# Two attentions, a quantised feed-forward network and an expert layer on one core: seven stages with a barrier between each, and the same stages in fewer blocks with their tiles interleaved

## The reference

```python
x = x + _L0_xattn_ref(_layernorm(x), ctx_768, Wq, bq, Wk, bk, Wv, bv, Wo, bo)      # 16 heads of 16
x = x + _L0_ffn_ref(_layernorm(x), w_gate, w_up, w_down)
x = x + _L1_xattn_ref(_layernorm(x), ctx_768, mask, g_norm, null_kv, Wq, Wkv, Wout, g_out)  # 16 heads of 64
x = x + _L1_ffn_ref(_layernorm(x), W, b, Wg, bg)                                   # 8 experts, top 2
```

```python
x = act_qdq(x)                              # scale = max|x| / 32767
up = act_qdq(x @ lpbq_dequant(w_up).T)
gate = act_qdq(x @ lpbq_dequant(w_gate).T)
sig = fixed_qdq_u16(jax.nn.sigmoid(gate))
gate = act_qdq(gate * sig)
o = act_qdq(gate * up)
return o @ lpbq_dequant(w_down).T
```

## Time and profile before

| | us |
|---|---|
| median of three runs | 1203.74 |
| the profiled execution | 1201.73 |
| its span in the profile | 1200.0 |
| PE busy | 1092.3 |
| DVE busy | 954.8 |
| ACT busy | 602.0 |
| POOL busy | 473.6 |

### The profile page before, as it was taken

One profiled execution on the slowest core, in us unless ns is written; L12 is line 12 of the kernel. 1 busy time (PEld: TensorE's weight loads), 2 busy tenths in 40 slices (PEclk: granted clock), 3 DMA queues, 4 the chain that ended last, 5 costly groups with the idle time before them and its releaser, 6 DMA issues. The chain is left out here.

```text
span 1200.0 us, 19905 instructions
## 1 busy us (share of the span) xinstructions
PE 1092.3 (91%) x6208; PEld 902.4 (75%) x6208; DVE 954.8 (80%) x2563; ACT 602.0 (50%) x1337; POOL 473.6 (39%) x546
## 2 busy tenths in 40 slices
PE   7899999996898885895997899999999969999997
PEld 5677777885786664442996898889989858888786
DVE  4688998886685989897664888988888759888886
ACT  1566766773555887586781333433433323333332
POOL 1245445432000757674000444555554434343433
PEclk9899999998899998687898999999999979999999
DMA  9000000000233686597204011011000000000000
GB/s 275 1 2 1 1 1 1 1 2 1 106 119 127 220 291 245 162 350 266 88 1 144 21 44 45 1 45 45 1 1 1 1 1 19 18 17 17 26 18 26
DMA packets 50048, 82.56 MB, mean 69 GB/s; under 512 B 4636, under 2 KB 35696, under 8 KB 49968
## 3 DMA queue, kind: packets, MB, share of 16 engines
q1 hardware_dynamic: 48591, 80.77, 19.9%
q10 hardware_dynamic: 1376, 0.79, 0.3%
HBM read 45.65 MB, written 35.90 MB: 68 GB/s over the span
## 5 line engine op out<-in xcount | busy, mean ns | idle before, releaser
L1134 PE MATMUL a_ps<-VW,a_PT 128*128 128x256 f32 x640 | 143.5, 379 | 0.0
L1134 PEld LDWEIGHTS a_ps<-VW,a_PT 128*128 128x128 f32 x640 | 120.2, 190 | 15.0
L1172 ACT ACTIVATE a_U<-a_U 128x1280 f32<-128x1280 f32 x32 | 40.7, 1271 | 110.7 <-DVE a_U L1257 110.7
L2245 POOL TENSOR_TENSOR m_half<-m_half 128x512 f32<-128x512 f32 x32 | 41.2, 1286 | 130.6 <-ACT m_half L2207 130.6
L1151 ACT COPY a_PT<-a_ps 128x512 f32<-128x512 f32 (+1 forms) x96 | 46.0, 517 | 82.6 <-PE a_ps L1097 82.6
L2147 PE MATMUL m_ps<-m_wh,m_xh 128*128 128x512 f32 x256 | 86.6, 420 | 0.0
L915 DVE TENSOR_SCALAR a_U<-a_ps 128x320 f32<-128x320 f32 x128 | 59.2, 484 | 32.8 <-PE a_ps L723 21.5
L1850 POOL TENSOR_SCALAR f_sg<-f_sg 128x1024 f32<-128x1024 f32 x24 | 36.7, 1529 | 113.6 <-ACT f_sg L1807 113.2
L2147 PE MATMUL m_ps<-m_wl,m_xh 128*128 128x512 f32 x256 | 80.9, 398 | 0.0
L1249 DVE TENSOR_REDUCE a_mx<-a_ps 128x4 f32<-128x320 f32 x128 | 62.4, 488 | 22.8 <-PE a_ps L1084 22.4
L2147 PE MATMUL m_ps<-m_wh,m_xl 128*128 128x512 f32 x256 | 80.6, 396 | 0.0
(11 more groups left out here) (257 smaller groups left out, 3179.6 us busy)
## 6 DMA issues: line engine op xcount, KB each, us to landing
up_scratch<-f_ub SPq DMA_DIRECT2D x24, 512.0 KB, 3.0
f_ul<-up_scratch SPq DMA_DIRECT2D x24, 512.0 KB, 5.5
key_scratch<-p_keys SPq DMA_DIRECT2D x8, 640.0 KB, 6.7
vw_scratch<-p_vw SPq DMA_DIRECT2D x16, 320.0 KB, 5.7
k_raw<-key_scratch SPq DMA_DIRECT2D x8, 640.0 KB, 6.1
VW<-vw_scratch SPq DMA_DIRECT2D x4, 1280.0 KB, 5.7
xs<-in_x SPq DMA_DIRECT2D x4, 1024.0 KB, 12.4
h_scratch<-f_hh SPq DMA_DIRECT2D x8, 512.0 KB, 2.7
```

Of the source, the lines that this page charges most:

```text
L1134: last = pe.matmul(Y[:, 0:D], PTs[t.p][:, j, :], fold.values[t.batch % 2][:, j, :], start=(j == 0), stop=(j == NJ - 1))
```

## The change

**Stages 4, 6 and 7 of the kernel become one block.** The last feed-forward stage, the second attention and the expert layer no longer write their programs themselves; each returns a `Stage` of generators, one for each engine, that yield after each step, and `finish` draws from them in an order given by hand. `d`, `a` and `m` are the three stages; the number is of steps.

```diff
+def finish(nc, down, att, experts):
...
+    with nc.Block() as block:
+        @block.sync
+        def _(sp):
+            down.sync(sp)
+            att.sync(sp)
+            experts.sync(sp)
+        @block.tensor
+        def _(pe):
+            d, a, m = down.tensor(pe), att.tensor(pe), experts.tensor(pe)
+            steps(d, 28)
+            steps(a, 3)
+            steps(d, 2)
+            steps(a, 1)
+            steps(d, 2)
+            steps(d)
+            steps(a, NT)
+            steps(m, 3)
+            steps(a, 1)
+            steps(m, 1)
+            steps(a)
+            steps(m)
...
+        @block.vector
+        def _(dve):
+            d, a, m = down.vector(dve), att.vector(dve), experts.vector(dve)
+            steps(d, 28)
+            steps(a, 2)
+            steps(d, 4)
+            steps(a, 1)
+            steps(d, 2)
+            steps(a, 1)
+            steps(d)
+            steps(a, 1 + NT - 2)
+            steps(m, 1)
+            steps(a, 1)
+            steps(m, 1)
+            steps(a, 1)
+            steps(m, 1)
+            steps(a, 1)
+            steps(m, 1)
+            steps(a)
+            steps(m)
```

**The down products** are written out on PE for all chunks. In the first chunk the units are outside and the token tiles inside, and the first unit goes through ACT and DVE in two halves:

```diff
+        def tensor(pe):
+            def down(t, j, u, ks):
+                for o_, w_ in ((oh, dTh), (ol, dTh), (oh, dTl)):
+                    for k in ks:
+                        lhs = o_[t % 2][:, u, k * CW + j * P:k * CW + (j + 1) * P]
+                        last = pe.matmul(Y[j][:, 0:D], lhs, w_[:, 2 * u + k, :],
+                                         start=(u == 0 and o_ is oh and w_ is dTh and k == 0),
+                                         stop=(u == UC - 1 and w_ is dTl and k == 1), skip_group_check=True)
+                return last
+            def ready(t, u):
+                pe.wait_ge(s_oh, UC * t + u + 1)
+                pe.wait_ge(s_ol, UC * t + u + 1)
+            pe.wait_ge(s_half[1], 1)
+            pe.wait_ge(s_half[2], 1)
                     for j in range(TC):
-                        if t.t0 >= 1:
-                            pe.wait_ge(s_x2, t.of(lambda n: TC * (n - 1) + j + 1))
-                        n = 0
+                down(0, j, 0, (0,))
+            ready(0, 0)
+            for j in range(TC):
+                down(0, j, 0, (1,))
+            for u in range(1, UC):
+                ready(0, u)
+                for j in range(TC):
+                    last = down(0, j, u, (0, 1))
+                    if u == UC - 1:
+                        last.then_inc(s_dn, 1)
+                        yield
+            for t in range(1, NCH):
+                for j in range(TC):
+                    pe.wait_ge(s_x2, TC * (t - 1) + j + 1)
                         for u in range(UC):
                             if j == 0:
-                                pe.wait_ge(s_oh, t.of(lambda n: UC * n + u + 1))
-                                pe.wait_ge(s_ol, t.of(lambda n: UC * n + u + 1))
-                            for o_, w_ in ((oh, dTh), (ol, dTh), (oh, dTl)):
-                                for k in (2 * u, 2 * u + 1):
-                                    lhs = o_[t.p][:, u, (k % 2) * CW + j * P:(k % 2) * CW + (j + 1) * P]
-                                    last = pe.matmul(Y[j][:, 0:D], lhs, w_[:, k, :], start=(n == 0),
-                                                     stop=(n == 3 * MF - 1))
-                                    n += 1
+                            ready(t, u)
+                        last = down(t, j, u, (0, 1))
                         last.then_inc(s_dn, 1)
-                pipeline(pe, body, 0, NCH - 1, 2, 5)
-    return fold
+                    yield
```

**Feed-forward stages 2 and 3 become one block**, and the folding runs one step ahead of the products. PE after the last up products:

```diff
+                def folded(m):
+                    p1.folded_key(pe, m, 0)
+                    p1.folded_key(pe, m, 1)
+                    if m == 1:
+                        pe.wait_ge(s_sc, SCALED)
+                    if m >= 1:
+                        p1.folded_value(pe, m - 1, 0)
+                    p1.folded_key(pe, m, 2)
+                    p1.folded_key(pe, m, 3)
+                    if m >= 1:
+                        p1.folded_value(pe, m - 1, 1)
+                pe.wait_ge(s_ue, MF * NCH)
+                p1.query_T(pe, 0, 0)
+                p1.query_T(pe, 0, 1)
+                p1.key_product(pe, 0)
+                p1.key_product(pe, 1)
+                p1.value_product(pe, 0)
+                folded(0)
                 rows_max(pe, 2)
                 rows_max(pe, 3)
                 spread_max(pe, 2)
                 spread_max(pe, 3)
+                for m in range(1, NM):
+                    p1.value_product(pe, m)
+                    if m + 1 < NM:
+                        p1.key_product(pe, m + 1)
+                    folded(m)
+                p1.folded_value(pe, NM - 1, 0)
+                p1.folded_value(pe, NM - 1, 1)
+                rows_max(pe, 4)
+                spread_max(pe, 4)
```

1537 lines of the change are left out of this document (810 added, 727 removed).

## The result

| us | before | after |
|---|---|---|
| median | 1205.09 (4 runs, 1201.26 to 1207.77) | 1176.84 (4 runs, 1173.82 to 1182.60) |
| profiled execution | 1201.73 | 1173.82 |
| its span | 1200.0 | 1172.1 |

What follows compares the result with a forecast made beforehand. PE was taken to bound the kernel, losing time at the seams between blocks. Six terms summed to -27.2 us, so 1174.5 for a profiled execution and, with 2.0 added for the median, 1176.5 us; range 1165 to 1190.

Steps and rivals of the forecast that it cites:

- term 6: Seam from second attention to experts: lost time regained except new waits of 4.0 and 2.8 us; -9.0 us, bounds -12 and -5.
- Rival A: Expert entry: the clock falls in the new 4.0 us wait; +3.5 us, 1180; chance 0.15.
- Term 3: Seam from stage 2 to 3 and all of stage 3: late maxima, less entry work, shorter tail; -2.7 us, bounds +4 and -7.
- rival B: Seam of stages 2 and 3 loses: maxima or value weights late, tail gives less; +7 us, 1183; chance 0.13.
- Term 4: Start of stage 4: halved first unit, barrier gone, less waiting in first chunk; -3.3 us, bounds -4.4 and -1.7.
- Term 5: Seam from stage 4 to second attention: overlap removes idle time and lower clock; -11.7 us, bounds -13.7 and -7.6.
- Terms 1 and 2: Masks moved behind tile 28 of the first attention, +1.5 us; stage 2's queue without value and output weight loads, -2.0 us.
- Rival C: Both seams give half, DVE being the bound or waits acting as barriers; 1187 us; chance 0.06.
- Rival D: Last feed-forward stage: 576 written-out matmuls issue more slowly than the loop's 0.121 us each; slower, 1210 us; chance 0.03.

Runs made afterwards that it cites:

- the combined kernel: Changed kernel with the expert entry reordered on POOL, DVE, PE and ACT, and the masks moved from tile 28 to tile 30; 1166.64 us, ratio to before 0.9695.

## Why the prediction was right or wrong

**The failed step is term 6**, the seam from the attention to the experts: -9.0 predicted, -1.1 measured, outside its own bounds of -12 and -5. "PE stands 4.0 us" was worked out from DVE's queue alone. I walked PE's and DVE's order, and took POOL's reciprocal root for one of the small operations, without asking what stands ahead of it in POOL's own program. There stood a whole step of attention tile 30, which waits for DVE: +2.4 us; with that step moved the wait was 3.57, within the 4.0 that I had counted. The second wait was 3.25 for 2.8, +0.5. Then the two clock drops, +4.6 us. Together 7.5 of the 7.9 missed. The prediction had named a sign for a wrong sum, over 10 us of idle time of PE at the two seams: it was 12.5 (2.8 and 9.7). So by its own test the sum is wrong, though the total agrees.

**Rival A**, the clock falling in that wait, came true, and the time was still the forecast's: the price I gave it (+3.5) for the first drop alone was near the 3.0 measured there (5.9 us of work at half the clock), but the second drop was not foreseen. What I held against it, that 0.5 us less would do, was wrong: it fell with 3.57 and with 3.25 us as well. It held through the 2.51 us of the kernel with the low halves moved, but also through 3.28 us in the kernel with the addition on POOL (1.00 in each microsecond from 960 to 968, the wait ending at 964.20), so the length of the wait alone does not tell. The 2.9 us that I read for the first seam are 2.8: a mean of 0.87 in the microsecond from 646 puts the fall at 646.74, against 643.97. In the same way the 2.4 us of the expectation for POOL's moved step are 2.0 (936.2 against 934.2). The total hit because terms 3 and 4 and the start gave more. That each wait is paid anew, as the Trainium skill has it (TensorE: Matmul & The Clock Gate, section HAM oscillation), the trace of after bears out twice in 20 us, and the wait of 3.28 us just named does not; here the wait is one for another engine, where the page's case is one for a DMA.

**Term 3**, stages 2 and 3: -2.7 predicted, -8.9 measured, outside the bound of -7. Its parts: the late maxima cost 3.0 and not 5.0; the value weights came in time, and rival B did not come. The tail gave its 4.1 exactly. The mis-sized part is the products. For the first seven I took the mean of before's products 8 to 24, 2.99 us, as a floor, where they came in 18.5 us, 2.64 each: -6.0 in place of -3.6. For the later ones I had 0; they gave -1.8, at (548.81-502.75)/16 = 2.88 each. But the kernel with the moved gain wait, whose code is that of before there, has 2.88 as well, so these 1.8 are not shown to be the change's. From the two profiles, masks of 1.9 us (the six DVE operations of the earlier trace rows) and some 1.4 us of the first folding step's masks, which now lie ahead of the maxima in stage 2, left DVE's program there; DVE's waits between the first and the last product went from 5.6 to 3.5 us, and the products themselves from 36.2 to 33.4. That makes 8.2 less, of which 7.8 arrive. The last part is not the change's: in the kernel with the moved gain wait the products take 34.1. This split is read, not tested; only the null copy was, and it shows no part in it. So why the products came faster than forecast stays open in part.

**Term 4**: -4.3 against -3.3. Two mistakes in opposite directions: the barrier did not go (+0.5), and the first chunk gave 2.9 where I had 0.9: besides the waiting that went, the clock was up 3.3 us after PE's start and not 7.8, which I had only as a doubt in the bounds (1.2 to 3.1 over all kernels, so that 2.9 is a good draw). The halves gave 1.5 for my 1.9.

**Term 5**: the last chunk and the entry gave -11.8 for -11.7, with 2.8 us of waits left as predicted; chunks 2 to 7 took 1.2 more, of which 0.80 is one wait at 570.04 for `f_o`. The size is right, the reason in part not. I put all of the lost time down to the missing overlap; 3.2 to 3.5 us of it were a load that POOL waited for, which a look at POOL's first row of that stage would have told.

**Terms 1 and 2**: +1.7 and -2.1, near +1.5 and -2.0. The second has the cause that I gave, ACT's waits for the stores of up, which went from 8.4 to 4.0 us. But I had only one side of it: up to the last product of the stage it is -3.9 (83.9 for 87.7; 83.4 to 86.3 in the nine other kernels with the queue of after), and the three mask operations of the first folding step, ahead of the maxima now, took 1.8 back (5.2 for 3.4). The masks stand on PE as one wait for DVE. Timeline of PE, before and then after:

```profile
275.00 0.81 PE L723 MATMUL a_ps<-keys,a_qT 64*128 64x320 f32 x4 [0.76 <-DVE a_U L915]
```

```profile
273.90 1.34 PE L842 MATMUL a_ps<-keys,a_qT 64*128 64x320 f32 x4 [2.30 <-DVE a_U L1034]
```

That is 1.5 us more, the forecast. The whole stretch grows by 1.8 between the kernels in which the clock falls early and stays low (227.1 and 228.8 to 228.9). In after the clock besides dips right behind this wait (mean 0.76 from 272 to 276 and 0.82 from 276 to 280), which none of the kernels without the masks there shows, but falls for good only 1.8 us ahead of the end of the stretch, where before had 5.6. So +1.7 is partly luck, and with masks the last tiles can grow by more than the 2 us that I had named as a sign of being wrong: 2.8 to 3.1 against before in three kernels. Moved to tile 30 the masks cost nothing: 227.0 in the combined kernel, where the clock falls early too.

**Rival C** (the seams give half) did not come: the second seam gave even less than its 5.0, and the first all that was forecast. **Rival D** is refuted: 54 written-out matmuls from 613.75 to 620.24 come every 0.120 us, and the loop of before had 0.121.

## What to carry to other kernels

Where two stages are woven together by hand, write down for the first tile of the new stage the whole chain over all engines, small operations too, and read for each link what stands ahead of it in that engine's queue; a 0.55 us operation, queued behind another tile's step on an engine with time to spare, made 2.9 of the 6.4 us that PE stood here. A wait for a load that stands ahead of a loop costs as much as one in it: before overlapping two stages, look at the first row of each engine in the second. And a total that agrees proves no term: cut both traces at the same instructions and compare stretch by stretch.

## What the runs showed of the hardware

**The tail of the first attention has two lengths, with the same code.** Its last tiles leave PE gaps of 0.5 to 1.5 us, and in some executions the clock falls there. Stretches of the kernel with the moved gain wait:

```profile
276.00:280.00 4.00, 2.52 (x20) 2.21 (x20) 1.72 (x8) 3.17 (x11) 1.27 (x2) 1.00 0.00 0
280.00:284.00 4.00, 4.00 (x25) 3.97 (x24) 1.18 (x4) 0.00 (x0) 0.00 (x0) 0.65 0.00 0
284.00:288.00 4.00, 3.27 (x14) 2.69 (x13) 1.31 (x6) 1.82 (x4) 1.28 (x2) 0.50 0.00 0
```

and of before, which has the same code there:

```profile
284.00:288.00 4.00, 3.10 (x26) 2.81 (x26) 1.64 (x7) 1.63 (x4) 1.28 (x2) 1.00 0.01 4
```

In before it fell only in the last tile. The rest of the first attention takes 221.8 us there, and 227.1 where it falls at 281. With the code of the change it takes 223.5 in after and 224.6 to 224.9 in three other kernels; in these four the clock dips for 3.4 to 6.8 us behind the masks, comes back, and falls for good 1.8 to 6.2 us ahead of the end of the stretch. It takes 228.8 to 228.9 in five kernels, in which the clock does not dip behind the masks but falls 19 us ahead of the end and stays low. These 5.3 us, with the 4.4 between the earliest and the latest start, are as wide as the spread of one kernel's runs (1173.82 to 1182.60 for after), and they are why the experiments are compared by stretches. What decides in which executions the clock falls, no run here tells.

**The clock can fall after the wait is over.** At the second seam it fell in the microsecond from 956, after PE had resumed at 955.93 from a wait of 3.25 us; in the kernel with POOL's step moved it fell in the microsecond from 943 after a wait of 3.57 us that had ended at 942.19. A clock of 1.00 in the wait itself thus does not say that the wait was harmless; the row behind it does. Nor does the same wait always end the same way: behind the 2.30 us that the masks cost in the first attention the clock dipped in after, and not behind 2.29 us in the kernel with the last block cut in two; behind the second wait of the expert entry (3.25 to 3.28 us) it fell in after and held in the kernel with the addition on POOL.
